# Five-layer graph network on one core: the counter update of a batch's products moves from the last product to a drain behind it

## What is computed

```python
# layer 0: sum of edge features per target node, then a two-layer perceptron
recv_agg = segment_sum(edge_attr, dst, n)
x += relu(concat(recv_agg, h, u) @ W1 + b1) @ W2 + b2
# layer 1: attention over edges, uses s_rel = edge_attr @ (w_r.T @ att_w[2d:])
x += relu(where(deg > 0, segment_sum(alpha * (h[src] + rh), dst, n) + h @ loop_w, h))
# layer 2: degree-weighted sums in both directions
agg_fwd = segment_sum(w * x[col], row, n); agg_bwd = segment_sum(w * x[row], col, n)
x += 0.5 * (agg_fwd @ W_src.T + b_src) + 0.5 * (agg_bwd @ W_dst.T + b_dst)
# layer 3: weighted mean over in-edges
ssum = segment_sum(edge_weight * node[src], dst, n); cnt = segment_sum(1, dst, n)
x += relu(layernorm(node + ssum / max(cnt, 1) @ W_rel.T + b_rel + node @ W_root.T) * gamma + beta)
```

## Time and profile before

| what | value |
|---|---|
| time, median of 3 runs | 9834.15 us (9824.49 to 9837.78) |
| span of the profiled execution | 9823.1 us |
| busy over the span | PE 7099.9, PEld 6078.6, DVE 6196.8, ACT 3293.8, POOL 4369.4 us |
| mean granted TensorE clock | 0.793 |

### The profile page before, as it was taken

One profiled execution on the slowest core, in us unless ns is written; L12 is line 12 of the kernel. 1 busy time (PEld: TensorE's weight loads), 2 busy tenths in 40 slices (PEclk: granted clock), 3 DMA queues, 4 the chain that ended last, 5 costly groups with the idle time before them and its releaser, 6 DMA issues. The chain is left out here.

```text
span 9823.1 us, 218886 instructions
## 1 busy us (share of the span) xinstructions
PE 7099.9 (72%) x59894; PEld 6078.6 (62%) x59895; DVE 6196.8 (63%) x20052; ACT 3293.8 (34%) x9071; POOL 4369.4 (44%) x5518
## 2 busy tenths in 40 slices
PE   5943004778967878878878797777797777696777
PEld 5843004765656666666657676667696766696666
DVE  7997004883346666666667676555786556786556
ACT  4722001333432222222223452000560002667785
POOL 0002772001036666666663355566465553465661
PEclk8955557999976666666667899888898887898987
DMA  0001003551123333333333586556686554686553
GB/s 21 2 2 29 10 9 87 150 149 46 38 59 87 86 86 85 87 86 88 87 85 115 198 287 215 164 166 161 245 338 186 164 163 134 253 338 183 166 166 117
DMA packets 640399, 1262.17 MB, mean 128 GB/s; under 512 B 121108, under 2 KB 179132, under 8 KB 639896
## 3 DMA queue, kind: packets, MB, share of 16 engines
q1 hardware_dynamic: 418919, 704.46, 21.3%
q0 software_dynamic: 199040, 544.46, 20.1%
q10 hardware_dynamic: 22196, 10.20, 0.4%
HBM read 780.96 MB, written 477.75 MB: 128 GB/s over the span
## 5 line engine op out<-in xcount | busy, mean ns | idle before, releaser
L1214 POOL DMA_INDIRECT GS<-t1d,KI x1564 | 1479.9, 946 | 1000.3 <-issue 380.3
L1106 PE MATMUL PS<-w,GS 128*128 128x128 f32 x6128 | 902.9, 313 | 319.2 <-DVE w L1005 251.4
L1106 PE MATMUL PS<-w,AREA 128*128 128x128 f32 x6048 | 860.6, 306 | 334.8 <-DVE w L1005 291.1
L1106 PEld LDWEIGHTS PS<-w,GS 128*128 128x128 f32 x6128 | 850.3, 223 | 371.7 <-DVE w L1005 294.1
L1106 PEld LDWEIGHTS PS<-w,AREA 128*128 128x128 f32 x6048 | 808.5, 215 | 385.2 <-DVE w L1005 333.5
L1005 DVE TENSOR_TENSOR w<-PS,KI 128x512 f32<-128x512 f32 x964 | 666.5, 691 | 316.9 <-issue 306.7
L2547 PE MATMUL PS<-AREA 128*128 128x128 bf16 x13392 | 842.7, 220 | 8.4 <-ACT GS L2473 4.6
L2547 PEld LDWEIGHTS PS<-AREA 128*128 128x128 bf16 x13392 | 792.0, 98 | 79.3 <-issue 6.1
L2522 DVE TENSOR_SCALAR AREA<-PS,w 128x1024 bf16<-128x1024 bf16 x558 | 715.9, 1284 | 161.2 <-PE PS L2533 161.2
L2491 POOL TENSOR_TENSOR AREA<-AREA,w 128x192 int32<-128x192 int32 x1116 | 528.3, 504 | 473.1 <-PE PS L2547 296.8
L2473 ACT ACTIVATE GS<-PS 128x1024 f32<-128x1024 f32 x558 | 571.3, 1024 | 315.2 <-PE PS L2547 300.0
(11 more groups left out here) (431 smaller groups left out, 14522.1 us busy)
## 6 DMA issues: line engine op xcount, KB each, us to landing
xbuf<-GS SPq DMA_DIRECT2D x558, 512.0 KB
XR<-in_edge_attr SPq DMA_DIRECT2D x780, 256.0 KB
pbuf<-AREA SPq DMA_DIRECT2D x482, 256.0 KB
GS<-t1d,KI POOLq DMA_INDIRECT x1564
AREA<-t2d ACTq DMA_DIRECT2D x121, 64.0 KB
GS<-xbuf,KI POOLq DMA_INDIRECT x484
keyd<-AREA POOLq DMA_INDIRECT x482
AREA<-xbuf,KI POOLq DMA_INDIRECT x480
```

The lines of the kernel that those rows point to most:

```text
L1106: i = e.matmul(PS[:, s % 3, 0:128], feats(s)[0:m, r, 0:D], SELW[s % 3][0:m, width * r:width * r + 128], start=(r == 0), stop=(r == 3))
L1214: e.indirect_dma_start(GS[0:m, s, r, 0:wide], None, table, bass.IndirectOffsetOnAxis(ap=idx[0:m, c:c + 1].bitcast(U32), axis=0)).then_inc( ...
```

## The change

In `unit`, the products no longer carry the update of `mmd`. A `drain` of TensorE is issued behind the batch's last product, and carries it. Waits and values of the counter stay the same, and so does the order of all other instructions. One drain per batch: 391 in layer 0's edge pass and 1,522 in the three summing passes.

```diff
                 for r in range(4):
-                    i = e.matmul(PS[:, s % 3, 0:128], feats(s)[0:m, r, 0:D], SELW[s % 3][0:m, width * r:width * r + 128],
+                    e.matmul(PS[:, s % 3, 0:128], feats(s)[0:m, r, 0:D], SELW[s % 3][0:m, width * r:width * r + 128],
                                  start=(r == 0), stop=(r == 3))
                 if count:
                     e.wait_ge(ohb, k)
                     for r in range(4):
-                        i = e.matmul(PS[:, s % 3, 128:128 + width], ONB[0:m, :], SELB[0:m, r, :],
+                        e.matmul(PS[:, s % 3, 128:128 + width], ONB[0:m, :], SELB[0:m, r, :],
                                      start=(r == 0), stop=(r == 3))
-                i.then_inc(mmd, 1)
+                e.drain().then_inc(mmd, 1)
                 e.reg_add(ku, ku, 1)
```

## The result

| what | before | after |
|---|---|---|
| time, median | 9829.32 us (9822.14 to 9837.78, 4 runs) | 12567.59 us (12564.11 to 12571.83, 4 runs) |
| ratio after to before, 95% interval | | 1.2794 (1.2776 to 1.2811) |
| span of the profiled execution | 9823.1 us | 12562.4 us |
| mean granted TensorE clock | 0.793 | 0.632 |
| busy over the span, PE / DVE / POOL | 7099.9 / 6196.8 / 4369.4 us | 8791.7 / 6349.1 / 4371.3 us |

The change makes the kernel 28% slower. The spans differ by 2,739 us, and that is what has to be found in the stages.

The account below looks back on a forecast made before the run. No engine was full; layer 0 waited on late updates, and TensorE's serial chain was to become the bound. Layer 0 −47 and summing passes +2,275 made +2,228 on 9,834: 12,060 us, range 10,500 to 12,750.

Parts of the forecast that it names:

- Parts 2 to 5: Summing batch: drain 0.05, exposed sequencer work 0.10 + 0.67, range load 0.19, products from empty array 2.07; 3.08 us at lower clock.
- part 3: Between batches, TensorE's formerly hidden sequencer instructions come into the open: 0.67 us plus 0.1 for the step after the drain.
- Part 6: TensorE's clock stays at the lower level in all four passes; summing passes 4,688 us against 2,413, +2,275.
- Part 7: Layer 0's pass: 3.22 us a batch, the 21 long waits gone if updates are on time; 1,259 us against 1,306, −47.
- rival B: Layer 0: the drain is held as well, so its first 660 us stay; +545 instead of −47, 12,650 us; chance 0.23.
- A: The forecast itself, all four passes: drain updates on time, lower clock; 12,060 us; chance 0.50.
- C: All four passes: the clock stays high, summing batch 2.17 us; 10,300 us, or 10,680 if layer 0 stays low; chance 0.16.
- D: Drain lets TensorE's sequencer go on, late updates vanish; layer 0 −622, summing passes −358, 8,850 us; chance 0.07.
- E: Nothing changes: the drain costs a few ns and the late updates remain, held by something else; chance 0.04.

Follow-up runs that it names:

- kernel with the counter ahead of the drain: The change with the raising of register ku moved from behind the drain to ahead of it; 12,434.93 us, ratio 1.2668.
- fill kernel: The change plus two float32 products of ones into an unused PSUM bank behind each summing-pass drain; 10,138.04 us, ratio 1.2268.
- both: The change with the update back on the last product and a bare drain behind it; 11,498.58 us in the first group of runs, 12,535.51 in the fourth.
- scatters first: The kernel before, with TensorE starting layer 0's pass only when all 482 scatters have landed; 9,788.08 us, ratio 0.9972.
- paced: The kernel before, with GpSimd's scatters spread over layer 0's pass by VectorE's batch counter; 9,405.12 us, ratio 0.9579.

## Why the prediction was right and wrong

**Parts 2 to 5, the batch of the summing passes: right.** 3.08 us were forecast. The timeline shows 2.05 us of products (2.07 taken), then 0.76 us until the next product, against 0.05 + 0.10 + 0.67 = 0.82; 2.81 in all. The stage average is 3.035, which leaves 0.22 for the load of ranges (0.19 taken). The passes came to 4,619 us instead of 4,688, so part 3 was some 0.06 us too large, well inside its bounds. The kernel with the counter ahead of the drain confirms that these instructions lie bare, at 0.1 us for one, and nothing where another takes its place. The fill kernel confirms the other price: 2.12 us at full clock, 2.17 forecast.

**Part 6, the clock: the level was right and is shown, the argument for it was weak.** Five stretches at 0.50. The row that it was argued from, a stretch of layer 1 with PE busy 90% at 0.50, decides nothing: the fill kernel's first summing pass has PE busy 1,022 of 1,183 us, 86%, and reads 1.00, and the kernel before's has 73% and reads 0.88. Two kernels separate the clock from the rest: with filler work the same drains cost 1,361 us less, with half the drains the clock reads 0.98. The Trainium skill (TensorE: Matmul & The Clock Gate, "Part 1: The HAM clock gate (the "warmup" mystery)") says that the clock depends on how busy TensorE has recently been; the fill kernel agrees, with 1.00 against 0.50 for the same waits.

**Part 7, layer 0: the size was right, the condition was wrong. This is the step that failed.** "If the drain's update is not late, the 21 long waits go and the pass is 391 × 3.22 = 1,259 us." The 1,259 was met where nothing is late (1,259.0 us) and where the scatters are paced (1,258 us). In the comparison the drains were held for 32.7 us, and rival B's sum holds: 660 + 370 × 3.22 = 1,851, measured 1,849. So layer 0's pass came 590 us above its term, +544 us and not −47. The measured time lies in the range only because the range had been drawn up to B; the forecast's own mechanism for layer 0 doesn't reach it. The other errors run the other way and hide a part of this one, 66 us in the summing passes and 14 us outside the changed stages: B's 9,834 + 2,820 = 12,654, less 66, 1 and 14, and less the 5 us by which the runs of before now came out lower, is 12,568, as measured.

**Why B was put at 0.23 and A at 0.50.** The argument was that products of later batches run on in the earlier trace rows while an update is out, so that only the message could be late. They do run on. But a product that streams doesn't show that the engine counts the earlier one as done, and a drain waits for just that. The bare drain of the fourth group of runs shows that a drain is held without a message of its own: for 32.8 us, in the same places as the product's update. The rule that was weighed pointed that way. The Trainium skill (PSUM — Partial Sum Buffer, "Engine vs sequencer instructions") has an attached update fire on completion, and a drain wait for an idle engine. From a late update that rule gives a late completion, and so a late drain, which is rival B. The prediction used it only to say that there would be nothing to win back. The runs fit the rule if completion itself is what comes late. That is inferred from update and drain being late in the same batches, and no row shows it. Against a single late event stands that the drain ends 2.1 us after the update. And in every kernel some instruction of the batch sends the update, so whether a drain is held where no update at all is under way was not tried.

**C fell** with the 0.50 of all stretches. Its 2.17 us was a good price for a clock that needs filler to be had. **D fell** because a drain does hold the sequencer. Its other half was right: without late updates layer 0's pass takes 685 us with the scatters beside it. **E fell** with the 28%; that the late updates stay was its true half.

**What is shown and what is open.** Shown: in layer 0's pass the updates of TensorE's products become late only where GpSimd's scatters run beside the pass (scatters first: none; paced: short ones). That they are let go when GpSimd pauses, as the expectation of the paced kernel had it, is not what the trace of the kernel before shows. Its scatters, and a late update that ScalarE waits for:

```profile
L1256 POOL DMA_INDIRECT keyd<-AREA x482: 954/958/1810, 907.8 to 1555.8; - x161
```

```profile
1577.23 0.36 ACT L1145 ACTIVATE w<-w 128x192 bf16<-128x192 f32 x1 [31.04 <-remote]
```

The last scatter was issued at 1555.8, and the update came 21 us later. Open: by what mechanism, whether the issuing or the transfers matter, and why a hold lasts 32 us with the scatters back to back and 4 us with them spread. What was not tried: pacing the indirect DMAs of layer 1.

## What to carry to other kernels

A drain of TensorE in a loop costs three times: the array runs empty, the sequencer's work for the next batch comes into the open, and the pauses can keep the engine at 1.2 GHz. Here the last was the largest (1,378 of 2,672 us where all was measured in one group of runs), so ask first whether the clock will hold, and drain every second batch if one must drain (that left an eighth of the loss). If an engine's updates come late, a drain behind them doesn't help: look for what runs beside them, and pace it; that gained 4.2% with one wait, on a kernel whose updates were late.

## What the runs showed of the hardware

**Two levels of one kernel.** The kernel before takes 8,265 us in one group of runs and 9,817 to 9,829 us in four. The kernel called both above ran in each kind, and its stages tell where the difference lies: layer 0's pass 1,250 against 1,841 us; the stages between it and the first summing pass 3,329 against 3,772; the summing passes 4,601 against 4,602. Without drains the summing passes differ as well, 1,929 against 2,410 us. So the drain hides there what the late updates cost, and is dearer where nothing is late. The stretch between, first where the kernel before takes 8,265 us, then where it takes 9,817:

```profile
2173.00:5502.00 3329.00, 2853.65 (x19384) 2194.88 (x19503) 2291.07 (x8837) 1202.14 (x3948) 1864.54 (x2308) 0.84 0.40 121
```

```profile
2763.00:6535.00 3772.00, 3151.80 (x19504) 2414.51 (x19503) 2295.77 (x8837) 1199.40 (x3948) 1859.98 (x2308) 0.74 0.35 107
```

POOL is busy to within 5 us of the same in both, so GpSimd's instructions are not what slows down. The record has the same chip number, 2, beside the first group of runs and beside the fourth, an hour later; if that is one chip, the level is not a property of the chip. What sets it the runs don't tell. It makes the change's ratio 1.28 or 1.39, as there are late updates in the time before or not.

**Late by 4 us or by 32.** With the scatters back to back (one every 1.3 us) a batch's update came 29 to 33 us behind its last product; with the same 482 scatters spread over the pass the longest wait was 4.4 us. In the kernel before, ScalarE goes on 33.60 us after the time before, 17 times in a row (the last at 1478.53, 1512.13 and 1545.73), though 26 or 27 scatters lie between two of these times at first and 24 later. So it isn't a number of scatters that lets an update go.

**Scatters cost the pass nothing where nothing is late.** Layer 0's pass took 685 us with 460 us of POOL's scatters beside it in the first group of runs, and 685 us with none beside it in the third.
